# Context attention: K's fp16 parts made with keys on partitions and turned by DMA

## The chip, the core and the metric

The kernel is one program on one NeuronCore of a Trainium2 chip. Its time is the device time of that core in microseconds (us). The engines are PE (matmuls, with PEld for its weight loads), DVE (VectorE), ACT (ScalarE), POOL (GpSimd) and SP, which here only issues DMAs. Each engine works off its own list of instructions strictly in order and waits on semaphores.

## The reference, cut to what matters

Two layers, each a cross attention from 64 latent rows to a long context, a self attention and a feed-forward part. The change touches the cross attention alone, which stands in both layers. For each of 16 batches, with 16 heads of 32 channels and 1585 context keys (the last 16 of 1601 take another path):

```python
q = _ln((x @ Wq + bq).reshape(b, s1, H, HD), qn_w, qn_b)      # 64 rows, 16 heads of 32
k = _ln((y_main @ Wk + bk) by head, kn_w, kn_b)               # 1585 keys
v = y_main @ Wv + bv by head
s = einsum('bhqd,bhkd->bhqk', q, k) * SCALE
ctx = einsum('bhqk,bhkd->bhqd', softmax(s), v)
```

All of it is float32. The kernel reaches that precision with pairs of fp16 numbers: a value is its rounding to fp16 ("high") plus the fp16 of what is left ("low").

## The kernel before, in words

`context_attention` runs over 16 batches. A batch's 1585 keys are 13 tiles of 128 (the last has 49). ORDER is a table written by hand that gives each engine its steps for one turn; `batches` walks it once per batch. A step's name is its kind and its tile, and each minus sign behind it moves it one batch back, so one turn mixes the projections of one batch with the attention of the batch before it. There is one turn per batch, and what sets the order is that table alone.

The steps of one tile, in the order in which they depend on each other:

- `yh` (ACT, L335) rounds the tile's context to fp16, `yl` (DVE, L411) subtracts to get the low part. Context comes to `l_land` by two loads a batch on SP's queue (L227, L230).
- `k` and `v` (PE, L545): six matmuls of 512 columns each into `ps_k` and `ps_v`, with keys on partitions.
- `kc` (DVE, L418) takes K out of PSUM with its bias, `sq` (ACT, L341) squares it, `rd` (DVE, L426) sums by head, and for two tiles at once `r` (ACT, L347, L351) and `nw` (POOL, L270 to L279) give the reciprocal root `rstd`.
- `hat` (POOL, L287) multiplies K by it into `khat`; `kt` (PE, L566) turns khat with four float32 transposes into `ps_kt`, so that channels are on partitions.
- `kh` (ACT, L356) and `kl` (DVE, L432) split `ps_kt` into the fp16 tensors `kh` and `kl`.
- `vh` (ACT, L362) and `vl` (DVE, L439) split V.

Then, by batch: `m0` to `m12` are rough scores (PE, L583) whose maxima DVE takes (L450); `t`, `tb`, `qs`, `qh`, `ql` put the maxima into the query; `s0` to `s13` are the exact scores (PE, L617), each followed by `e` (ACT, L382 and L384: two exponentials, one to float32 and one to fp16), `lo` (POOL, L307: the difference of the two) and `pv` (PE, L641 to L645: the products with V). `m0` waits for the fp16 K of the first four tiles, `m4` and `m8` for four more each, `m12` and `s0` for all.

A wait by step: `kt` of a tile waits for `kl` of the tile before (there is one `ps_kt`), `k` for `kc` of the tile before, `v` for `vl` of it. A projection waits for the `yl` of its tile.

Of the kernel before, what the change touches and what calls it, by code (L numbers as in the profile page):

```python
# [38 lines left out]
YA = 6  # L39
# [14 lines left out]
    ACT: e9- sq11- kh7- e10- yh0 kh8- r5- vh11- e11- sq12- kh9- e12- yh1 kh10- e13- vh12- r6- kh11- sq0 yh2
    ACT: vh0 vh1 yh3 kh12- sq1 vh2 yh4 r0 sq2 qh- vh3 sq3 yh5 e0 vh4 yh6 sq4 kh0 r1 e1 vh5 yh7 sq5 kh1 e2 yh8
    ACT: vh6 sq6 r2 kh2 e3 vh7 sq7 kh3
    DVE: kc8- rd7- kl4- yl9- m0- vl8- kc9- rd8- kl5- rd9- yl10- m1- o0- vl9- kc10- yl11- rd10- kl6- m2- kc11-
    DVE: vl10- kl7- m3- yl12- rd11- kl8- m4- vl11- kc12- m5- rd12- kl9- yl0 m6- yl1 kl10- m7- kc0 vl12- kl11-
    DVE: m8- rd0 m9- vl0 yl2 kc1 m10- vl1 yl3 m11- kc2 rd1 m12- t- vl2 kc3 qs- yl4 kl12- ql- vl3 yl5 rd2 kc4
# [22 lines left out]
def context_attention(nc, env, ctx_dram, qs_dram, wk, wv, bk, wo_x_raw, dca_dram):  # L82
# [7 lines left out]
    with ExitStack() as ctx:  # L90
# [130 lines left out]

        with nc.Block() as block:

            @block.sync
            def _(sp):
                def load_a(b):
                    sp.dma_start(y[:, :, 0:YA * P], ctx_dram[b, :, :, 0:YA * P]).then_inc(y_a, 16)  # L227

                def load_b(b):
                    sp.dma_start(y[:, :, YA * P:MAIN], ctx_dram[b, :, :, YA * P:MAIN]).then_inc(y_b, 16)  # L230

                def load_q(b, bp):
                    sp.dma_start(q0[:, bp].rearrange("p g q -> p (g q)"), qs_dram[b]).then_inc(q_in[bp], 16)

                load_a(0)
                load_b(0)
                load_q(0, 0)
# [3083 lines left out]
```

## Time and profile before

| | |
|---|---|
| time, median of 3 runs | 3381.3 us (3379.84 to 3383.14) |
| span of the profiled execution | 3386.0 us |
| PE busy | 3119.5 us, 92% |
| DVE busy | 2655.1 us, 78% |
| ACT busy | 2269.3 us, 67% |
| POOL busy | 1864.8 us, 55% |

No time of the profiled execution other than its span is recorded; the span lies 4.7 us over the median of the runs. Shares are over the whole program; the two context attentions take about two thirds of it, and there the engines are busier than these shares say. The trace models the end of a matmul, and neighbouring matmuls overlap in it, so the time that a step of PE really takes is read from its start to the start of what follows. On DVE and ACT too the recorded end of an instruction lies a little behind the start of the next. Below, such a distance from start to start is called a slot.

### The profile page before, as it was taken

Reading aid. Unit: us, or ns where it says so; the run is one execution under the profiler, and the core shown is the slowest. Engines: PE = TensorE matmul, PEld = TensorE weight load, DVE = VectorE, ACT = ScalarE, POOL = GpSimd, SP = SyncE. Lnnn points to the kernel's source line nnn. Section 1 sums busy time; section 2 is a strip of 40 time slices with the busy share of each in tenths; the row PEclk is TensorE's granted clock in tenths of the full one; section 3 lists DMA queues with packets and bytes.
Section 4 is the critical chain, followed back from the end, with each engine's and each line's share of the span. In section 5 each row is a group of like instructions: output and inputs, shape, how many; then the busy total and the mean of one; then the engine's idle time right before and its main releaser. Section 6 shows DMA issues by size and latency. Waiting matters only on the chain. (4 is left out here: it accounts for less than half of the span.)

```text
span 3386.0 us, 89189 instructions
## 1 busy us (share of the span) xinstructions
PE 3119.5 (92%) x35753; PEld 1945.5 (57%) x35753; DVE 2655.1 (78%) x4082; ACT 2269.3 (67%) x4027; POOL 1864.8 (55%) x2294
## 2 busy tenths in 40 slices
PE   7799999999999968879996899999999999987889
PEld 4356665666556646667773346556655665564546
DVE  6688888888888855768875688888888888866752
ACT  5478887888788755346664468788877887774431
POOL 1267776777677742212224257677767777662310
PEclk9899999999999979989998899999999999987989
DMA  3110010101010033358884301010101001001010
GB/s 121 61 34 23 23 33 24 32 23 33 23 34 23 28 114 125 109 184 278 302 305 128 92 22 33 23 34 23 33 23 34 23 23 33 23 21 54 1 68 25
DMA packets 102368, 223.67 MB, mean 66 GB/s; under 512 B 35445, under 2 KB 47861, under 8 KB 96202
## 3 DMA queue, kind: packets, MB, share of 16 engines
q1 hardware_dynamic: 93994, 190.71, 16.9%
q0 software_dynamic: 7680, 25.17, 2.5%
q8 instruction: 289, 4.73, 0.6%
q10 hardware_dynamic: 288, 2.10, 0.1%
q14 instruction: 117, 0.96, 0.1%
HBM read 181.86 MB, written 36.09 MB: 64 GB/s over the span
## 5 line engine op out<-in xcount | busy, mean ns | idle before, releaser
L307 POOL TENSOR_TENSOR a_elo<-a_e 128x1024 f16<-128x1024 f32 x428 | 867.3, 2026 | 160.6 <-ACT a_e L384 159.6
L545 PE MATMUL a_ps_k<-l_wk,a_yh 128*128 128x512 f16 (+1 forms) x1664 | 568.3, 382 | 31.4 <-DVE a_yl L411 27.4
L545 PE MATMUL a_ps_v<-l_wv,a_yh 128*128 128x512 f16 (+1 forms) x1664 | 568.0, 382 | 19.1 <-DVE a_v L439 19.1
L450 DVE TENSOR_REDUCE a_mx<-a_ps_m 128x2 f32<-128x1024 f32 x384 | 466.7, 1215 | 13.0 <-PE a_ps_m L583 12.8
L382 ACT ACTIVATE a_e<-a_ps_t 128x1024 f32<-128x1024 f32 x428 | 410.9, 960 | 98.2 <-PE a_ps_t L617 91.8
L287 POOL TENSOR_TENSOR a_khat<-a_kc,a_rstd 128x512 f32<-128x512 f32 (+1 forms) x416 | 443.7, 1073 | 16.5 <-PE a_ps_kt L566 6.0
L384 ACT ACTIVATE a_e<-a_ps_t 128x1024 f16<-128x1024 f32 x428 | 410.7, 960 | 0.0
L411 DVE TENSOR_TENSOR a_yl<-l_land,a_yh 128x256 f16<-128x256 f32 (+1 forms) x416 | 352.0, 847 | 19.3 <-ACT a_yh L335 19.0
L418 DVE SCALAR_TENSOR_TENSOR a_kc<-a_ps_k,l_bk 128x512 f32<-128x512 f32 (+1 forms) x416 | 284.0, 683 | 91.6 <-PE a_ps_k L545 91.2
L641 PE MATMUL a_ps_o<-a_v,a_e 128*128 128x65 f16 (+1 forms) x3240 | 344.6, 194 | 10.4 <-POOL a_elo L307 10.4
L432 DVE SCALAR_TENSOR_TENSOR a_kl<-a_ps_kt,a_kh 128x512 f16<-128x512 f32 (+1 forms) x416 | 274.1, 659 | 91.2 <-ACT a_kh L356 91.2
L643 PE MATMUL a_ps_o<-a_v,a_e 128*128 128x64 f16 (+1 forms) x3240 | 343.1, 194 | 0.0
L356 ACT ACTIVATE a_kh<-a_ps_kt,a_one 128x512 f16<-128x512 f32 (+1 forms) x416 | 277.0, 666 | 96.5 <-PE a_ps_kt L566 96.4
L645 PE MATMUL a_ps_o<-a_v,a_elo 128*128 128x65 f16 (+1 forms) x3240 | 341.3, 193 | 0.0
L439 DVE SCALAR_TENSOR_TENSOR a_v<-a_ps_v,a_v 128x512 f16<-128x512 f32 (+1 forms) x416 | 284.6, 684 | 70.7 <-ACT a_v L362 68.4
L362 ACT ACTIVATE a_v<-a_ps_v 128x512 f16<-128x512 f32 (+1 forms) x416 | 246.7, 593 | 125.2 <-PE a_ps_v L545 125.2
L617 PE MATMUL a_ps_t<-a_qb,a_kh 64*128 64x128 f16 (+1 forms) x6448 | 323.9, 218 | 6.5 <-DVE a_qb L474 5.0
L641 PEld LDWEIGHTS a_ps_o<-a_v,a_e 128*128 128x128 f16 (+1 forms) x3240 | 297.8, 96 | 53.5 <-ACT a_e L384 23.1
L545 PE MATMUL a_ps_v<-l_wv,a_yl 128*128 128x512 f16 (+1 forms) x832 | 316.6, 381 | 0.0
L545 PE MATMUL a_ps_k<-l_wk,a_yl 128*128 128x512 f16 (+1 forms) x832 | 316.3, 380 | 0.0
L341 ACT ACTIVATE a_sq<-a_kc 128x512 f32<-128x512 f32 (+1 forms) x416 | 262.5, 631 | 68.5 <-DVE a_kc L418 68.5
L545 PEld LDWEIGHTS a_ps_k<-l_wk,a_yh 128*128 128x128 f16 (+1 forms) x1664 | 163.1, 98 | 249.7 <-issue 55.0
(428 smaller groups left out, 6807.2 us busy)
## 6 DMA issues: line engine op xcount, KB each, us to landing
l_ob<-in_m_w SPq DMA_DIRECT2D x32, 1024.0 KB, 8.0
l_land<-in_ctx SPq DMA_DIRECT2D x32, 817.0 KB, 5.0
l_land<-in_ctx SPq DMA_DIRECT2D x32, 768.0 KB, 4.7
f_w<-in_m_w SPq DMA_DIRECT2D x32, 512.0 KB, 4.8
eo_dram<-f_e_eo SPq DMA_DIRECT2D x32, 512.0 KB, 4.4
qs_dram<-p_q SPq DMA_DIRECT2D x32, 128.0 KB, 2.4
dca_dram<-p_od SPq DMA_DIRECT2D x16, 256.0 KB, 2.4
a_q<-qs_dram SPq DMA_DIRECT2D x32, 128.0 KB, 2.0
```

The costliest lines, as they stand in the source:

```text
L287: pool.tensor_tensor(khat[0:r, t, :].rearrange("p (h d) -> p h d", d=HD), kc[0:r, kc_slot(at, i), :].rearrange("p (h d) -> p h d", d=HD), ...
L307: pool.tensor_tensor(rest[0:r, :, 0:w], full[0:r, :, 0:w], high[0:r, :, 0:w], ALU.subtract)\
L382: act.activation(full[0:r, :, 0:w], src[0:r, :, 0:w], ACT.Exp)
L384: act.activation(high[0:r, :, 0:w], src[0:r, :, 0:w], ACT.Exp).then_inc(e_done, 1)
L411: dve.tensor_tensor(yl[:, t, :, 0:r], y[:, :, i * P:i * P + r], yh[:, t, :, 0:r], ALU.subtract).then_inc(yl_done, 1)
L439: dve.scalar_tensor_tensor(out=v[0:r, at.nbp, i, :, 66:130], in0=ps_v[0:r, :].rearrange("p (a d) -> p a d", d=64), scalar=1.0 / WSCALE, in ...
L450: dve.tensor_reduce(mx[:, g, :, c], ps_m[:, :, :], AX.X, ALU.max).then_inc(mx_done, 1)
L545: m = pe.matmul(out[0:r, :], part[:, t, c, 0:r], w[:, wpart, c, :], start=(c == 0 and a == 0), stop=(c == KC - 1 and a == 2))
L617: t = pe.matmul(dst[0:rows(i), r, col:col + P], kpart[d, at.bp, g, k], qb[d, at.bp, g, qpart, :, :].rearrange("p a q -> p (a q)"), start=( ...
L641: pe.matmul(ps_o[:, a * OW:a * OW + OW], high[k, r, col], v[k, at.bp, i, pair, 0:OW], start=first, stop=False, skip_group_check=True)
L643: pe.matmul(ps_o[:, a * OW:a * OW + 64], high[k, r, col], v[k, at.bp, i, pair, 66:130], start=False, stop=False, skip_group_check=True)
L645: t = pe.matmul(ps_o[:, a * OW:a * OW + OW], rest[k, r, col], v[k, at.bp, i, pair, 0:OW], start=False, stop=last, skip_group_check=True)
```

## The change

K's path is made anew; the other steps compute what they did.

- `hat` moves from POOL to DVE (L467 of the changed kernel). It multiplies `kc` in SBUF by the reciprocal root in PSUM and writes to PSUM: `ps_h`, which takes the place of `ps_kt`, with keys still on partitions. A new step `rp` on ACT (L384) first copies a tile's 16 reciprocal roots into the last 16 columns of `ps_h`.
- `kh` and `kl` split `ps_h` into `khl`, two buffers of [128 keys, high and low, 512 channels].
- `kt` is gone. SP issues for each tile one DMA transpose of 256 KB (64 rows for the last tile) from `khl` into `kk`, which holds high and low K with channels on partitions. `m` and `s` read `kk`, and wait for the transposes to land (`wait_turned`). `kh` of a tile waits until the transpose of two tiles before has landed; the first transpose of a batch also waits for the last scores of the batch two before.
- The split of the context (`yh`, `yl`) goes by four chunks of three tiles (the last has four), on ACT and now POOL instead of ACT and DVE: L361 and L316. The loads go by the same four chunks. A chunk's buffer is free once the V projections of the chunk two before are done.
- All four orders are written anew.

```diff
-KCOLS = MAIN + MAIN % 2
+KCOLS = -(-MAIN // 64) * 64
+RSTD = D - H
...
+CHUNKS = 4
+PER = KT // CHUNKS
+WIDEST = MAIN - (CHUNKS - 1) * PER * P + 1
...
-    PE: pv11- s13- m7- k0 kt11- pv12- pv13- m8- v0 m9- k1 m10- v1 k2 m11- kt12- v2 m12- k3 tb- v3 k4 s0 v4
+    PE: s12-- k2- pv11-- m8-- v12-- m9-- s13-- pv12-- m10-- v0- pv13-- m11-- k3- m12-- v1- tb-- k4- v2- s0-
...
+    ACT: rp11-- vh10-- r6-- kh11-- sq0- e11-- vh11-- rp12-- sq1- e12-- kh12-- r0- vh12-- e13-- yh1- sq2- rp0-
...
+    DVE: m0- kl5- kc9- hat6- rd8- m1- kc10- kl6- rd9- hat7- rd10- kl7- m2- kc11- hat8- vl7- o0- rd11- m3- kl8-
...
-        yh = sb("yh", [P, 2, KC, P], F16)
-        yl = sb("yl", [P, 2, KC, P], F16)
-        kh = sb("kh", [P, 2, GROUPS, KCOLS], F16)
-        kl = sb("kl", [P, 2, GROUPS, KCOLS], F16)
+        yh = sb("yh", [P, 2, KC, WIDEST], F16)
+        yl = sb("yl", [P, 2, KC, WIDEST], F16)
+        khl = sb("khl", [P, 2, 2, D], F16)
+        kk = sb("kk", [P, 2, 2 * GROUPS, KCOLS], F16)
...
-        ps_kt = ps("ps_kt", [P, GROUPS, P])
+        ps_h = ps("ps_h", [P, 512])
...
+        def chunk_free(eng, n):
+
+            if n >= 2:
+                b, c = divmod(n - 2, CHUNKS)
+                eng.wait_ge(v_done, b * KT + (KT if c == CHUNKS - 1 else (c + 1) * PER))
+
+        def wait_turned(eng, tiles):
+
+            for k in range(2):
+                n = len(range(k, tiles, 2))
+                if n:
+                    eng.wait_ge(turned[k], 16 * n)
...
+                def load(b, c):
+                    lo, hi = chunk_columns(c)
+                    sp.dma_start(y[:, :, lo:hi], ctx_dram[b, :, :, lo:hi]).then_inc(y_in[c], 16)
+
+                def load_q(b):
+                    sp.dma_start(q0[:, b % 2].rearrange("p g q -> p (g q)"), qs_dram[b]).then_inc(q_in[b % 2], 16)
+
+                def turn(b, i):
+                    n, r = b * KT + i, -(-rows(i) // 64) * 64
+                    sp.wait_ge(kl_done, n + 1)
+                    if i == 0 and b >= 2:
+                        sp.wait_ge(s_done, (b - 1) * UNITS)
+                    sp.dma_start_transpose(kk[:, b % 2, :, i * P:i * P + r],
+                                           khl[0:r, n % 2].rearrange("p a d -> p (a d)")).then_inc(turned[n % 2], 16)
+
+                for c in range(CHUNKS):
+                    load(0, c)
+                    if c == 0:
+                        load_q(0)
+                        load_q(1)
+                for b in range(B):
+                    for i in range(KT):
+                        if i % PER == 1 and i // PER < CHUNKS and b + 1 < B:
+                            sp.wait_ge(yl_done, b * CHUNKS + i // PER + 1)
+                            load(b + 1, i // PER)
+                        turn(b, i)
+                    if 1 <= b < B - 1:
+                        sp.wait_ge(q1_done, b)
+                        load_q(b + 1)
...
+                    need(pool, rp_done, at.nb * KT + 2 * p - 2 + (p == 0))
                     pool.tensor_tensor(rstd[0:r, u, 0:nt, :], r2, a2, ALU.mult).then_inc(newton[4], 1)
 
-                def hat(at, i):
-
-                    n, t, r, p = at.nb * KT + i, tile_par(at.nbp, i), rows(i), i // 2
-                    u = (at.nbp * TPAIRS + p) % 2
-                    pool.wait_ge(newton[4], at.nb * TPAIRS + p + 1)
-                    need(pool, kt_done, n - 1)
-                    pool.tensor_tensor(khat[0:r, t, :].rearrange("p (h d) -> p h d", d=HD),
-                                       kc[0:r, kc_slot(at, i), :].rearrange("p (h d) -> p h d", d=HD),
-                                       rstd[0:r, u, i % 2, :].unsqueeze(2).broadcast_to([r, H, HD]), ALU.mult)\
-                        .then_inc(hat_done, 1)
+                def y_low(at, c):
+                    n = at.nb * CHUNKS + c
+                    lo, hi = chunk_columns(c)
+                    pool.wait_ge(yh_done, n + 1)
+                    chunk_free(pool, n)
+                    pool.tensor_tensor(yl[:, n % 2, :, 0:hi - lo], y[:, :, lo:hi], yh[:, n % 2, :, 0:hi - lo],
+                                       ALU.subtract).then_inc(yl_done, 1)
...
+                def root_in(at, i):
+
+                    n, r, p = at.nb * KT + i, rows(i), i // 2
+                    act.wait_ge(newton[4], at.nb * TPAIRS + p + 1)
+                    need(act, kl_done, n)
+                    act.activation(ps_h[0:r, RSTD:D], rstd[0:r, (at.nbp * TPAIRS + p) % 2, i % 2, :], ACT.Copy)\
+                        .then_inc(rp_done, 1)
+
                 def k_high(at, i):
                     n, r = at.nb * KT + i, rows(i)
-                    act.wait_ge(kt_done, n + 1)
-                    act.activation(kh[:, at.nbp, :, i * P:i * P + r], ps_kt[:, :, 0:r], ACT.Identity, bias=one[:, 0:1])\
+                    act.wait_ge(hat_done, n + 1)
+                    if n >= 2:
+                        act.wait_ge(turned[n % 2], 16 * (n // 2))
+                    act.activation(khl[0:r, n % 2, 0, :], ps_h[0:r, :], ACT.Identity, bias=one[0:r, 0:1])\
                         .then_inc(kh_done, 1)
...
-                def y_low(at, i):
-                    n, t, r = at.nb * KT + i, tile_par(at.nbp, i), rows(i)
-                    dve.wait_ge(yh_done, n + 1)
-                    dve.tensor_tensor(yl[:, t, :, 0:r], y[:, :, i * P:i * P + r], yh[:, t, :, 0:r],
-                                      ALU.subtract).then_inc(yl_done, 1)
...
+                def hat(at, i):
+
+                    n, r = at.nb * KT + i, rows(i)
+                    dve.wait_ge(rp_done, n + 1)
+                    dve.tensor_tensor(ps_h[0:r, :].rearrange("p (h d) -> p h d", d=HD),
+                                      kc[0:r, kc_slot(at, i), :].rearrange("p (h d) -> p h d", d=HD),
+                                      ps_h[0:r, RSTD:D].unsqueeze(2).broadcast_to([r, H, HD]), ALU.mult)\
+                       .then_inc(hat_done, 1)
...
+                    dve.scalar_tensor_tensor(out=khl[0:r, n % 2, 1, :], in0=ps_h[0:r, :], scalar=1.0,
+                                             in1=khl[0:r, n % 2, 0, :], op0=ALU.add, op1=ALU.subtract)\
...
                 def project(at, i, out, w, done):
-                    t, r = tile_par(at.nbp, i), rows(i)
+                    c, r = chunk_of(i), rows(i)
+                    n = at.nb * CHUNKS + c
+                    pe.wait_ge(yl_done, n + 1)
+                    cols = slice((i - c * PER) * P, (i - c * PER) * P + r)
                     steps = [(yh, 0), (yl, 0), (yh, 1)]
                     for c in range(KC):
...
-                def k_turned(at, i):
-                    n, t = at.nb * KT + i, tile_par(at.nbp, i)
-                    pe.wait_ge(hat_done, n + 1)
-                    need(pe, kl_done, n)
-                    for g in range(GROUPS):
-                        m = pe.transpose(ps_kt[:, g, :], khat[:, t, g * P:(g + 1) * P], ident[:, :])
-                    m.then_inc(kt_done, 1)
-
                 def first_scores(at, m):
 
                     c, g = divmod(m, GROUPS)
-                    pe.wait_ge(kh_done, at.nb * KT + min(4 * c + 4, KT))
+                    wait_turned(pe, at.nb * KT + min(4 * c + 4, KT))
...
-                                          kh[q, at.nbp, g, o:o + w], start=True, stop=True)
+                                          kk[q, at.nbp, g, o:o + w], start=True, stop=True)
...
-                        pe.wait_ge(kl_done, at.b * KT + KT)
+                        wait_turned(pe, at.b * KT + KT)
```

PE (rows as the program has them, before), layer 0, where the last rough scores of a batch stand among projections of the next; a_ps_kt is K being turned, a_ps_m the rough scores, a_ps_k and a_ps_v the projections:

```order
L583 MATMUL a_ps_m<-a_kh,a_qm 128x512 x2
L566 MATMUL a_ps_kt<-ident,a_khat 128x128 x4
L545 MATMUL a_ps_v<-l_wv,a_yh 128x512
L545 MATMUL a_ps_v<-l_wv,a_yl 128x512
L545 MATMUL a_ps_v<-l_wv,a_yh 128x512 x2
L545 MATMUL a_ps_v<-l_wv,a_yl 128x512
L545 MATMUL a_ps_v<-l_wv,a_yh 128x512
L583 MATMUL a_ps_m<-a_kh,a_qm 128x49 x8
```

The same place in the change, m11, k3, m12 of its order:

```order
L617 MATMUL a_ps_m<-a_kk,a_qm 128x512 x2
L591 MATMUL a_ps_k<-l_wk,a_yh 128x512
L591 MATMUL a_ps_k<-l_wk,a_yl 128x512
L591 MATMUL a_ps_k<-l_wk,a_yh 128x512 x2
L591 MATMUL a_ps_k<-l_wk,a_yl 128x512
L591 MATMUL a_ps_k<-l_wk,a_yh 128x512
L617 MATMUL a_ps_m<-a_kk,a_qm 128x49 x8
```

The four transposes have gone, and the projection that stands there is k3, the first that reads the second chunk of the context.

DVE before, from m9 to m11 of a batch; a_yl is the low context:

```order
L450 TENSOR_REDUCE a_mx<-a_ps_m 128x2
L439 SCALAR_TENSOR_TENSOR a_v<-a_ps_v,a_v 128x8x64
L411 TENSOR_TENSOR a_yl<-l_land,a_yh 128x256
L418 SCALAR_TENSOR_TENSOR a_kc<-a_ps_k,l_bk 128x512
L450 TENSOR_REDUCE a_mx<-a_ps_m 128x2
L439 SCALAR_TENSOR_TENSOR a_v<-a_ps_v,a_v 128x8x64
L411 TENSOR_TENSOR a_yl<-l_land,a_yh 128x256
L450 TENSOR_REDUCE a_mx<-a_ps_m 128x2
```

DVE in the change, from the last hat of a batch on; a_ps_h is the normed K, a_khl its low part:

```order
L467 TENSOR_TENSOR a_ps_h<-a_kc,a_ps_h 49x512
L493 TENSOR_REDUCE a_mx<-a_ps_m 128x2
L475 SCALAR_TENSOR_TENSOR a_khl<-a_ps_h,a_khl 49x512
L493 TENSOR_REDUCE a_mx<-a_ps_m 128x2
L482 SCALAR_TENSOR_TENSOR a_v<-a_ps_v,a_v 49x8x64
L452 SCALAR_TENSOR_TENSOR a_kc<-a_ps_k,l_bk 128x512
L493 TENSOR_REDUCE a_mx<-a_ps_m 128x2
L467 TENSOR_TENSOR a_ps_h<-a_kc,a_ps_h 128x512
L493 TENSOR_REDUCE a_mx<-a_ps_m 128x2
L482 SCALAR_TENSOR_TENSOR a_v<-a_ps_v,a_v 128x8x64
L475 SCALAR_TENSOR_TENSOR a_khl<-a_ps_h,a_khl 128x512
```

The subtractions of the context have left DVE, and a multiplication for each tile has come in front of each low part, with one or two other instructions between the two.

SP before, one batch; a_q is the query:

```order
L233 DMA a_q<-qs_dram 128x256
L227 DMA l_land<-in_ctx 128x2x768
L230 DMA l_land<-in_ctx 128x2x817
L233 DMA a_q<-qs_dram 128x256
L227 DMA l_land<-in_ctx 128x2x768
```

SP in the change, one batch:

```order
L263 DMA_TRANSPOSE a_kk<-a_khl 128x8x128
L253 DMA l_land<-in_ctx 128x2x384
L263 DMA_TRANSPOSE a_kk<-a_khl 128x8x128 x3
L253 DMA l_land<-in_ctx 128x2x384
L263 DMA_TRANSPOSE a_kk<-a_khl 128x8x128 x3
L253 DMA l_land<-in_ctx 128x2x384
L263 DMA_TRANSPOSE a_kk<-a_khl 128x8x128 x3
L253 DMA l_land<-in_ctx 128x2x433
L263 DMA_TRANSPOSE a_kk<-a_khl 128x8x128 x2
L263 DMA_TRANSPOSE a_kk<-a_khl 128x8x64
L256 DMA a_q<-qs_dram 128x256
```

Thirteen transposes have come into the queue of the loads, which stand between them.

## Rows read from the trace of the kernel before

**Rows 1.** the page: the span and the busy time of each engine

```profile
span 3386.0 us, 89189 instructions
...
PE 3119.5 (92%) x35753; PEld 1945.5 (57%) x35753; DVE 2655.1 (78%) x4082; ACT 2269.3 (67%) x4027; POOL 1864.8 (55%) x2294
```

**Rows 2.** windows, one turn: busy us PE, PEld, DVE, ACT, POOL; clock, DMA

```profile
501.70:570.24 68.54, 67.43 (x897) 40.66 (x897) 59.71 (x89) 54.37 (x97) 51.06 (x64) 1.00 0.09 28
```

**Rows 3.** timeline of PE: start us, us, engine, line, op, shapes, count

```profile
513.10 0.38 PE L545 MATMUL a_ps_k<-l_wk,a_yh 128*128 128x512 f16 x1
...
514.49 0.39 PE L583 MATMUL a_ps_m<-a_kh,a_qm 64*128 64x512 f16 x2
514.81 0.65 PE L566 MATMUL a_ps_kt<-ident,a_khat 128*128 128x128 f32 x4
515.30 0.38 PE L545 MATMUL a_ps_v<-l_wv,a_yh 128*128 128x512 f16 x1
```

**Rows 4.** timeline of PE, same turn: the longest and the shortest transpose step

```profile
523.99 0.60 PE L566 MATMUL a_ps_kt<-ident,a_khat 128*128 128x128 f32 x4
524.67 0.38 PE L545 MATMUL a_ps_k<-l_wk,a_yh 128*128 128x512 f16 x1
...
532.82 0.60 PE L566 MATMUL a_ps_kt<-ident,a_khat 128*128 128x128 f32 x4
533.25 0.19 PE L641 MATMUL a_ps_o<-a_v,a_e 128*128 128x65 f16 x1
```

**Rows 5.** timeline of PE where the last batch of layer 0 starts its scores

```profile
1204.49 0.39 PE L617 MATMUL a_ps_t<-a_qb,a_kh 64*128 64x128 f16 x4 [2.48 <-DVE a_qb L474]
```

**Rows 6.** the score line L617: count, duration ns min/median/max, first and last start us

```profile
L617 PE MATMUL a_ps_t<-a_qb,a_kh x6448: 216/216/312, 179.2 to 3049.2; 64*128 64x128 f16 x179, 64*49 64x128 f16 x17
```

**Rows 7.** DVE over that turn by line: count, busy us, mean ns, idle before

```profile
L450 DVE TENSOR_REDUCE a_mx<-a_ps_m 128x2 f32<-128x1024 f32 x13 | 15.8, 1215 | 0.3 <-PE a_ps_m L583 0.3
L411 DVE TENSOR_TENSOR a_yl<-l_land,a_yh 128x256 f16<-128x256 f32 (+1 forms) x13 | 11.4, 876 | 0.0
...
L432 DVE SCALAR_TENSOR_TENSOR a_kl<-a_ps_kt,a_kh 128x512 f16<-128x512 f32 (+1 forms) x13 | 8.6, 659 | 2.7 <-ACT a_kh L356 2.7
```

**Rows 8.** ACT over the same turn, by line

```profile
L384 ACT ACTIVATE a_e<-a_ps_t 128x1024 f16<-128x1024 f32 (+1 forms) x15 | 14.4, 962 | 0.0
...
L335 ACT ACTIVATE a_yh<-l_land 128x256 f16<-128x256 f32 (+1 forms) x13 | 5.3, 408 | 1.6 <-PE a_ps_v L545 1.6
...
L351 ACT ACTIVATE a_r<-a_lnv 128x32 f32<-128x32 f32 (+1 forms) x7 | 1.6, 227 | 0.6
```

**Rows 9.** POOL over the same turn, by line

```profile
L307 POOL TENSOR_TENSOR a_elo<-a_e 128x1024 f16<-128x1024 f32 (+1 forms) x14 | 28.3, 2023 | 3.8 <-ACT a_e L384 3.8
L287 POOL TENSOR_TENSOR a_khat<-a_kc,a_rstd 128x512 f32<-128x512 f32 (+1 forms) x14 | 15.1, 1085 | 0.3
```

**Rows 10.** timeline of DVE: L411 beside a POOL instruction and alone, with what follows

```profile
571.00 2.16 DVE L411 TENSOR_TENSOR a_yl<-l_land,a_yh 128x256 f16<-128x256 f32 x1
573.08 0.68 DVE L432 SCALAR_TENSOR_TENSOR a_kl<-a_ps_kt,a_kh 128x512 f16<-128x512 f32 x1
...
580.13 0.41 DVE L411 TENSOR_TENSOR a_yl<-l_land,a_yh 128x256 f16<-128x256 f32 x1
580.46 0.68 DVE L418 SCALAR_TENSOR_TENSOR a_kc<-a_ps_k,l_bk 128x512 f32<-128x512 f32 x1
581.06 1.21 DVE L450 TENSOR_REDUCE a_mx<-a_ps_m 128x2 f32<-128x1024 f32 x1
```

**Rows 11.** timeline of POOL at the first of the two

```profile
570.75 2.12 POOL L307 TENSOR_TENSOR a_elo<-a_e 128x1024 f16<-128x1024 f32 x1
```

**Rows 12.** DMA issues of the page: count, KB each, median us to landing

```profile
qs_dram<-p_q SPq DMA_DIRECT2D x32, 128.0 KB, 2.4
dca_dram<-p_od SPq DMA_DIRECT2D x16, 256.0 KB, 2.4
```

**Rows 13.** DMA issues by line, further down: another transfer of 256 KB

```profile
h_dram<-f_h SPq DMA_DIRECT2D x8, 256.0 KB, 12.2
```

More of the change, by code:

```diff
@@ L54 @@
[L54 to L59, printed above, removed]
@@ L60 @@
-    DVE: rd3 o1- vl4 yl6 kc5 kl0 rd4 vl5 rd5 kl1 yl7 kc6 vl6 kl2 rd6 kc7 yl8 vl7 kl3
-    POOL: hat4- lo3- hat5- lo4- nw3- lo5- hat6- lo6- hat7- lo7- nw4- lo8- hat8- lo9- hat9- lo10- nw5- hat10-
-    POOL: lo11- hat11- lo12- lo13- nw6- hat12- qm nw0 hat0 hat1 lo0 nw1 lo1 hat2 hat3 lo2 nw2
+    PE: k12-- v8-- pv7-- s9-- m4-- pv8-- v9-- k0- s10-- m5-- v10-- k1- pv9-- m6-- s11-- v11-- pv10-- m7--
+    PE: s12-- k2- pv11-- m8-- v12-- m9-- s13-- pv12-- m10-- v0- pv13-- m11-- k3- m12-- v1- tb-- k4- v2- s0-
@@ new lines @@
+    ACT: r4- kh7- e7-
+    DVE: kc2- m10-- hat0- m11-- vl0- kl0- m12-- t-- kc3- rd2- qs-- vl1- rd3- hat1- ql-- kc4- kl1- vl2- kc5-
+    DVE: hat2- rd4- vl3- kl2- o1-- kc6- rd5- hat3- vl4- rd6- kl3- kc7- hat4- vl5- rd7- kl4- kc8- hat5- vl6-
+    DVE: m0- kl5- kc9- hat6- rd8- m1- kc10- kl6- rd9- hat7- rd10- kl7- m2- kc11- hat8- vl7- o0- rd11- m3- kl8-
+    DVE: kc12- vl8- hat9- m4- kl9- vl9- hat10- kc0 m5- kl10- rd12- hat11- vl10- kc1 kl11- m6- rd0 m7- vl11-
+    DVE: rd1 hat12- m8- kl12- m9- vl12-
@@ L63 @@
+    POOL: nw0- lo13-- yl1- nw1- yl2- qm- lo0- lo1- nw2- lo2- yl3- lo3- nw3- lo4- lo5- lo6- nw4- lo7- lo8- yl0
+    POOL: nw5- lo9- lo10- nw6- lo11- lo12-
 """
@@ L134, in context_attention @@
         ps_o = ps("ps_o", [P, 512])
-        y_a, y_b, const_ok, ones_ok = sem("y_a"), sem("y_b"), sem("const_ok"), sem("ones_ok")
+        const_ok, ones_ok = sem("const_ok"), sem("ones_ok")
+        y_in = [sem(f"y_in{c}") for c in range(CHUNKS)]
         q_in = [sem("q_in0"), sem("q_in1")]
@@ L171, in context_attention @@
         e_sets = [(e32[:, t], e16[:, t], elo[:, t]) for t in range(2)]
-        for t, spare in enumerate((khat, sq)):
-            halves = spare[:, :, :].bitcast(F16).rearrange("p t (u n) -> p (t u) n", n=512)
-            e_sets.append((kc[:, 2 * t:2 * t + 2], halves[:, 0:2], halves[:, 2:4]))
+        halves = sq[:, :, :].bitcast(F16).rearrange("p t (u n) -> p (t u) n", n=512)
+        e_sets.append((kc[:, 0:2], khl[:, 0], khl[:, 1]))
+        e_sets.append((kc[:, 2:4], halves[:, 0:2], halves[:, 2:4]))
         def e_set(at, j):
@@ L213, in batches @@
         def batches(name, attention, step):
-            for turn in range(-2, B + 1):
+            for turn in range(-2, B + 2):
                 for kind, i, shift in STEPS[name]:
@@ L225, in _ @@
             def _(sp):
[L226 to L237, printed above, removed]
@@ L312, in step @@
                         newton_step(at, i)
-                    elif kind == "hat":
-                        hat(at, i)
+                    elif kind == "yl":
+                        y_low(at, i)
                     elif kind == "qm":
@@ L361, in v_high @@
                     act.wait_ge(v_done, n + 1)
+                    if i == 0 and at.nb >= 2:
+                        act.wait_ge(pv_done, 2 + (at.nb - 1) * UNITS)
                     act.activation(v[0:r, at.nbp, i, :, 0:64], ps_v[0:r, :].rearrange("p (a d) -> p a d", d=64),
@@ L392, in step @@
                         guess(at, i)
+                    elif kind == "rp":
+                        root_in(at, i)
                     elif kind == "kh":
@@ L508, in step @@
                 def step(kind, i, at):
-                    if kind == "yl":
-                        y_low(at, i)
-                    elif kind == "kc":
+                    if kind == "kc":
                         k_centred(at, i)
+                    elif kind == "hat":
+                        hat(at, i)
                     elif kind == "rd":
@@ L544, in project @@
                         for a, (part, wpart) in enumerate(steps):
-                            m = pe.matmul(out[0:r, :], part[:, t, c, 0:r], w[:, wpart, c, :],
+                            m = pe.matmul(out[0:r, :], part[:, n % 2, c, cols], w[:, wpart, c, :],
                                           start=(c == 0 and a == 0), stop=(c == KC - 1 and a == 2))
@@ L653, in step @@
                         v_product(at, i)
-                    elif kind == "kt":
-                        k_turned(at, i)
                     elif kind == "m":
```

60 lines of the change are left out of this document (22 added, 38 removed).

## The prediction

> **What bounds the kernel now.** I read the busy shares first, then one turn of a context attention, then the slots of PE in it. Over the program PE is busy 92% of 3386.0 us [rows 1]. In one turn of layer 0 (68.54 us) PE is busy 67.43 us at the full granted clock of 1.00, DVE 59.71, ACT 54.37 and POOL 51.06 [rows 2]. So PE sets the pace and DVE comes 13% behind it. The length of a turn is fixed from outside too: the first exact scores start at 179.2 us [rows 6] and those of the last batch at 1204.49 [rows 5], 15 turns apart, so 68.35 us each. Two layers make 30 such turns, 2050 of the 3386 us. What one turn gains counts 30 times; the rest of the program is untouched but for the filling and draining of each attention.
>
> **PE: the transposes go.** A transpose step (four float32 matmuls) takes from its start to the next start 0.49 us in the middle of projections (514.81 to 515.30) [rows 3], at most 0.68 and at least 0.43 [rows 4]. The 13 of the turn have a mean of 0.51, so 13 x 0.51 = 6.6 us go from PE (5.6 and 8.8 if all were like the shortest or the longest). Nothing replaces them on PE: the matmuls of k, v, m, s and pv are the same in number and shape. If every other wait of PE stayed, a turn would be 68.35 - 6.6 = 61.7 us. The matmuls of a k step take 1.39 us up to the next start (513.10 to 514.49) and an m step 0.32 [rows 3].
>
> **DVE: subtraction out, multiplication in.** Thirteen subtractions leave, 11.4 us [rows 7], some 10.4 without the overlaps of about 0.08 us between neighbours. They are dear because POOL holds them up: alone one has a slot of 0.33 us (580.13 to 580.46), but the one that starts at 571.00 takes until 573.08 [rows 10], while POOL's 570.75 instruction runs for 2.12 us [rows 11]. Thirteen multiplications of 512 columns with PSUM on one side come in. The nearest row is kc, also 512 columns from PSUM with a second operand in SBUF: a slot of 0.60 us (580.46 to 581.06) [rows 10], so 7.8 us. The other end is a multiplication held up as the subtractions are, 0.876 us each [rows 7], 11.4 us. I take 0.60. DVE then has 59.7 - 10.4 + 7.8 = 57.1 us of work in a turn of some 62 to 63, 91% against 87% now.
>
> The trace's pair of subtractions shows the hold-up by its 0.33 and 2.08 us. The Trainium skill (SBUF — State Buffer, "Who interferes with whom") says that a DVE instruction with two inputs in SBUF contends with a GpSimd instruction that reads SBUF, and one with a single SBUF input doesn't; the trace agrees for the subtraction, and the multiplication is of the second kind, since the roots are copied to PSUM. By this rule it costs 0.60; without it the 0.876 would stand, 3.6 us a turn more on DVE.
>
> **ACT and POOL.** ACT loses 13 roundings, 5.3 us (4.3 without overlaps). It gains four of 768 to 866 columns, which by the exponential of 1024 columns in 0.962 us [rows 8] are 0.75 to 0.85 each, 3.1 in all, and 13 copies of 16 columns, bounded by zero and by the 0.227 us of a 32-column instruction [rows 8]: 2.5. ACT goes from 54.4 to 55.7 us. POOL loses khat (15.1 us for the 14 that fall in the window [rows 9], 14.1 for 13) and gains 3170 columns of subtraction, at 2.12 us for 1024 [rows 11] 6.6 us: 43.6 us. Neither sets a turn, but both stand in chains.
>
> **A new wait of PE: k3.** The second chunk of the context may be rounded only when the V projections of tile 12 of the batch before are done, and k3 needs its low part. In ACT's order the rounding yh1 stands behind e13, in POOL's yl1 behind lo13. From the end of v12 PE has m9, s13, pv12, m10, v0, pv13, m11 before k3; three m at 0.32 and v0 at 1.3 make 2.3, and the two pv and s13 come to some 1.7: 4.0 us. The other side: s13 ends at 0.8, two exponentials of half size (by 0.962 for a full one, some 0.55 each) end at 2.0, lo13 (half of 2.12) at 3.2, yl1 (768 columns, 1.6) at 4.8, and a semaphore later PE may go on, at about 5.0. So PE waits 1.0 us once a turn; the bounds are 0 and 2. Before k0 and k6 and k9 the same sum leaves PE no wait.
>
> **The transposes.** The trace has none; its price is bounded by other DMAs. Below: 256 KB of plain rows land in 2.4 us, and 128 KB in 256-byte pieces also in 2.4 [rows 12]. A transpose moves 1024 pieces of 256 bytes, twice as many, so between 2.4 and 4.8 by these two. Above: another 256 KB transfer took 12.2 us [rows 13], eight of them queued behind each other. I take 3.5, in the middle of the near rows. Who waits: kh of a tile waits for the transpose of two tiles before, and a tile comes every 62.8 / 13 = 4.8 us, so two buffers leave about 9.6 less the 1.5 of kh and kl, 8 us. Tighter are the rough scores. Between kl3 and the maximum m0, DVE has eight instructions with a slot of about 0.60, 4.8 us; less PE's own m0 (0.3) and a semaphore, the transpose may take 4.3 us. Between kl11 and m8 the same count gives 4.3; before m4 and m12, 7 and 6. At 3.5 none is late, but the margin is under one microsecond at two places. Behind a late m on PE stand the exact scores and behind these the exponentials, so a late transpose counts in full. Behind a waiting transpose on SP stand only loads that are due a whole turn later; their four 400 KB transfers a turn are issued between transposes.
>
> How the chip treats a transpose no row here can show. The Trainium skill says of the crossbar that "TRN2 transpose DMAs are as fast as regular DMAs" (Advanced Engine Details and Errata, "X-Bar Transpose (TRN2)"), which would be 2.4 us by our plain row and leave the sum as it is. The same page calls the transpose efficiency of hardware descriptor generation "Worse" than that of the software way ("DGE: Hardware vs Software") and gives no figure; this is the kind used here, and it speaks for the slower rival below.
>
> **The sum.** A turn: 68.35 - 6.6 + 1.0 = 62.8 us, 5.6 less (I round up); 30 turns, -168 us. The ends: filling is nearest to DVE's work, which falls by 2.6 us in each layer, -5; in draining the last transpose must land before m12, +3.5 in each, +7. Together -166, from 3386.0 to 3220 of span. The profiled execution lies 4.7 us over the median of the runs, so I forecast 3215 us.
>
> **Rivals.**
> - *DVE and the chains take over.* A tile of K now goes ACT, DVE, ACT, DVE through the one ps_h: copy, multiply, round, subtract, four handovers where before there were three. If DVE keeps the 8.8 us of idle time that it has in a turn now [rows 2], a turn is 57.1 + 8.8 = 65.9, 2.5 less: 3386 - 75 - 5 = 3306. For it: kl waits 2.7 us a turn for kh [rows 7], and three engines stand near 90% at once. Against it: much of that idle time is there because PE is late, and the new order puts one or two instructions between hat and kl. A multiplication that is held up by POOL (3.6 us) would end here too.
> - *Transposes land late: slower.* The place is PE before m0 and m8, then m4 and m12. With a landing time of L us each turn pays (L - 4.3) twice, (L - 5.9) and (L - 7.2) where positive. That eats the gain of 5.6 at L = 6.7; at 8 it is 10.3, so 4.7 a turn longer: 3381 + 141 = 3522. At 12.2 it would be about 27 a turn, and the ring of two buffers alone would give (1.2 + 12.2) / 2 x 13 = 87 us a turn: about 3940. For it: 416 transposes through one queue, pieces of 256 bytes, loads in between. Against it: DMA engines are busy 9% in a turn now [rows 2].
> - *PE loses its other waits too.* The order is new, k3 needn't wait, and PE's 1.1 us of idle time [rows 2] goes: 68.35 - 6.6 - 1.1 = 60.7, 7.7 less: 3381 - 231 = 3150. It needs DVE at 94%.
>
> **How the numbers follow.** Forecast 0.50 (3180 to 3260: 61.7 to 64.3 a turn); DVE and chains 0.18, near 3306; no other waits 0.10, near 3150; late transposes 0.22, of which 0.19 slower than before and 0.03 level with it. So faster by over 0.2% 0.78, within 0.2% (about what runs of this kernel can tell from no change) 0.03, slower 0.19. The range from 3155 to 3350 leaves out most of the late transposes (0.16) and a little below (0.03).
>
> **What would show it.** A turn of 62.8 us between the first exact scores of two batches; no float32 transposes on PE; the multiplication at 0.60 us a slot; POOL's subtraction of a chunk near 1.6 us; a wait of about 1 us before k3 for POOL; transposes that land in 3 to 4 us, and no wait of m for a DMA. It is wrong if m or kh waits for transposes by microseconds, if DVE is over 93% busy, or if the turn is over 65 us with PE idle for DVE or ACT.

## The result, and the profile after

The changed kernel takes 3176.5 us (median of 4 runs, 3169.9 to 3177.5) against 3382.2 us for the kernel before on the same chip: a ratio of 0.9382, 95% interval 0.937 to 0.9393, 206 us faster. The forecast was 3215 in a range of 3155 to 3350. The measured time lies in the range, but 3.5 us below the band of 3180 to 3260 that the forecast gave its own mechanism. In a later group of runs the same kernel gave 0.9374 (0.9361 to 0.9386). The span of the profiled execution is 3175.6 us, 210.4 less than before [rows 1].

The page of the changed kernel, its span and busy times, the answer to [rows 1]:

```profile
span 3175.6 us, 86675 instructions
...
PE 2894.2 (91%) x34089; PEld 1765.8 (56%) x34089; DVE 2585.9 (81%) x4082; ACT 2282.1 (72%) x4155; POOL 1619.6 (51%) x2006
```

One turn of its layer 0, the answer to [rows 2] (length, busy us and count of PE, PEld, DVE, ACT, POOL, clock, DMA share, GB/s):

```profile
547.24:608.40 61.16, 59.97 (x845) 35.06 (x844) 57.07 (x89) 54.73 (x100) 43.35 (x54) 1.00 0.46 85
```

The first exact scores of the first and of the last batch of layer 0, which fix the length of 15 turns as [rows 5, 6] do for before:

```profile
183.17 0.84 PE L651 MATMUL a_ps_t<-a_qb,a_kk 64*128 64x128 f16 x24 [0.43 <-DVE a_qb L517]
```

```profile
1100.69 1.46 PE L651 MATMUL a_ps_t<-a_qb,a_kk 64*128 64x128 f16 x24 [2.48 <-DVE a_qb L517]
```

A turn is (1100.69 - 183.17) / 15 = 61.17 us, where it was 68.35. (Most turns are 61.30 us from first score to first score, where they were 68.54; the last of a layer is shorter.) Thirty turns give 7.18 x 30 = 215 us, and 5 are given back at the ends: the first scores start 4.0 us later than before (183.2 against 179.2). DVE's 57.07 and POOL's 43.35 us are the forecast's 57.1 and 43.6; ACT has 54.73, forecast 55.7.

The lines of DVE in that turn that answer to [rows 7], and of ACT and POOL to [rows 8, 9]:

```profile
L493 DVE TENSOR_REDUCE a_mx<-a_ps_m 128x2 f32<-128x1024 f32 x12 | 14.6, 1218 | 0.2 <-PE a_ps_m L617 0.2
...
L467 DVE TENSOR_TENSOR a_ps_h<-a_kc,a_ps_h 128x512 f32<-128x512 f32 (+1 forms) x13 | 8.9, 687 | 1.8 <-ACT a_ps_h L384 1.7
L475 DVE SCALAR_TENSOR_TENSOR a_khl<-a_ps_h,a_khl 128x512 f16<-128x512 f32 (+1 forms) x13 | 8.9, 681 | 0.6 <-ACT a_khl L392 0.4
```

```profile
L361 ACT ACTIVATE a_yh<-l_land 128x768 f16<-128x768 f32 (+1 forms) x4 | 3.4, 860 | 0.0
L384 ACT ACTIVATE a_ps_h<-a_rstd 128x16 f32<-128x16 f32 (+1 forms) x13 | 2.5, 189 | 1.9 <-DVE a_khl L475 1.9
```

```profile
L317 POOL TENSOR_TENSOR a_yl<-l_land,a_yh 128x768 f16<-128x768 f32 (+1 forms) x4 | 6.5, 1637 | 0.8 <-ACT a_yh L361 0.7
```

The multiplication costs 687 ns, like kc. The order's extra instruction between hat and kl shows too: DVE waits 0.4 us a turn for kh, where it waited 2.7 [rows 7]. It now waits 1.7 for the copies of the roots; in all it is idle for 4.1 us of the turn, where it was for 8.8 [rows 2]. The DMA issues of the page, which answer to [rows 12, 13], have the transposes in them:

```profile
a_kk<-a_khl SPq DMA_TRANSPOSE x416, 3.1
qs_dram<-p_q SPq DMA_DIRECT2D x32, 128.0 KB, 2.3
dca_dram<-p_od SPq DMA_DIRECT2D x16, 256.0 KB, 2.4
```

A transpose of 256 KB lands after a median of 3.1 us (2.7 to 5.3 over 416 of them), 0.7 more than the plain transfer. It takes the DMA engines longer than that suggests: they are busy 46% of the turn against 9%, with 85 GB/s against 28. No m of the turn waits for one. From the end of kl to the m that needs it the trace has 5.9 us before m0 (561.4 to 567.3), where the forecast counted 4.3; 4.5 before m8 (594.4 to 598.9), where it counted 4.3; and 6.7 and 5.8 before m4 and m12, where it had 7 and 6. So only m8 is tight. The place in PE's order where the forecast saw a new wait (start, length, what, and the idle time with its releaser):

```profile
543.49 0.39 PE L617 MATMUL a_ps_m<-a_kk,a_qm 64*128 64x512 f16 x2
544.24 0.38 PE L591 MATMUL a_ps_k<-l_wk,a_yh 128*128 128x512 f16 x1 [0.36 <-POOL a_yl L317]
```

k3 does wait for POOL's yl1, but 0.4 us, not 1.0.

### The profile page after: what moved, and what is told of

Its sections match the earlier page's. It is cut to its first block and busy times, and to the rows that moved or that the text cites. A ratio compares the mean times of both kernels' runs of the same rounds, so it can differ in the third digit from the quotient of the medians.

```text
span 3175.6 us, 86675 instructions
## 1 busy us (share of the span) xinstructions
PE 2894.2 (91%) x34089; PEld 1765.8 (56%) x34089; DVE 2585.9 (81%) x4082; ACT 2282.1 (72%) x4155; POOL 1619.6 (51%) x2006
## 5 line engine op out<-in xcount | busy, mean ns | idle before, releaser
L335 POOL TENSOR_TENSOR a_elo<-a_e 128x1024 f16<-128x1024 f32 x428 | 852.9, 1996 | 301.4 <-ACT a_e L422 297.7
L651 PE MATMUL a_ps_t<-a_qb,a_kk 64*128 64x128 f16 (+1 forms) x9672 | 350.5, 218 | 23.0 <-DVE a_qb L517 20.2
L675 PEld LDWEIGHTS a_ps_o<-a_v,a_e 128*128 128x128 f16 (+1 forms) x3240 | 298.6, 96 | 98.5 <-issue 61.5
L651 PEld LDWEIGHTS a_ps_t<-a_qb,a_kk 64*128 64x128 f16 (+1 forms) x9672 | 286.4, 95 | 103.7 <-DVE a_qb L517 35.4
L467 DVE TENSOR_TENSOR a_ps_h<-a_kc,a_ps_h 128x512 f32<-128x512 f32 (+1 forms) x416 | 285.8, 687 | 58.1 <-ACT a_ps_h L384 55.7
L677 PEld LDWEIGHTS a_ps_o<-a_v,a_e 128*128 128x128 f16 (+1 forms) x3240 | 299.8, 97 | 24.8
L392 ACT ACTIVATE a_khl<-a_ps_h,a_one 128x512 f16<-128x512 f32 (+1 forms) x416 | 284.0, 683 | 33.1 <-DVE a_ps_h L467 32.1
L679 PEld LDWEIGHTS a_ps_o<-a_v,a_elo 128*128 128x128 f16 (+1 forms) x3240 | 300.2, 99 | 0.0
L475 DVE SCALAR_TENSOR_TENSOR a_khl<-a_ps_h,a_khl 128x512 f16<-128x512 f32 (+1 forms) x416 | 283.4, 681 | 19.2 <-ACT a_khl L392 12.6
```

The source lines that it names most:

```text
L335: pool.tensor_tensor(rest[0:r, :, 0:w], full[0:r, :, 0:w], high[0:r, :, 0:w], ALU.subtract)\
L392: act.activation(khl[0:r, n % 2, 0, :], ps_h[0:r, :], ACT.Identity, bias=one[0:r, 0:1])\
L467: dve.tensor_tensor(ps_h[0:r, :].rearrange("p (h d) -> p h d", d=HD), kc[0:r, kc_slot(at, i), :].rearrange("p (h d) -> p h d", d=HD), ps_h ...
L651: t = pe.matmul(dst[0:rows(i), r, col:col + P], kk[d, at.bp, kpart + g, k], qb[d, at.bp, g, qpart, :, :].rearrange("p a q -> p (a q)"), st ...
L675: pe.matmul(ps_o[:, a * OW:a * OW + OW], high[k, r, col], v[k, at.bp, i, pair, 0:OW], start=first, stop=False, skip_group_check=True)
L677: pe.matmul(ps_o[:, a * OW:a * OW + 64], high[k, r, col], v[k, at.bp, i, pair, 66:130], start=False, stop=False, skip_group_check=True)
```

## The experiments

All times are compared through their ratio to the kernel before on the same chip, with the changed kernel at 0.9374 to 0.9382. One per cent is 34 us. "Over 15 turns" means from the first exact scores of the first batch of layer 0 to those of its last, as above.

**PE's transposes put back.** In `k_product` of the changed kernel:

```diff
                     need(pe, kc_done, at.nb * KT + i)
+                    for g in range(GROUPS):
+                        pe.transpose(ps_k[:, g * P:(g + 1) * P], ident[:, :], ident[:, :])
                     project(at, i, ps_k, wk, k_done)
```

> The changed kernel with four float32 transposes of the identity put on PE in front of every k step, into ps_k, where the matmuls of k overwrite them: PE gets back what it lost and nothing else changes. Theory (PE sets the pace of a turn, and its transposes were the gain): 13 x 0.5 = 6.6 us a turn, 30 turns, about +200 us, so 3360 to 3390, the time before. Rival (part of the gain comes from DVE's dear subtractions having gone, and PE has slack): under +130 us, below 3310.

Measured: 3331.0 us, ratio 0.9827 (0.981 to 0.9843), 151 us slower than the changed kernel: between the two, nearer to the rival. One turn of it:

```profile
513.45:579.86 66.41, 66.11 (x897) 41.20 (x897) 57.65 (x89) 55.34 (x100) 43.52 (x54) 1.00 0.41 78
```

Over 15 turns a turn is 66.18 us, 5.0 longer than the changed kernel's. Its k steps, with the transposes in them, take 6.1 us more slots than the changed kernel's (23.6 against 17.5 us), and PE's idle time shrinks by 0.9 us (1.2 to 0.3). With as many transposes as before, PE still finishes a turn 2.2 us earlier than in the kernel before (68.35); up to 0.5 of that may be the transposes themselves, which took 6.6 us of slots there.

**The kernel before with its transposes doubled.**

```diff
-                    for g in range(GROUPS):
+                    for g in (0, 1, 2, 3, 0, 1, 2, 3):
```

> The kernel before with every K tile turned twice on PE, eight transposes instead of four: if a turn was bound by PE alone, 13 x 0.45 to 0.51 = 5.9 to 6.6 us a turn, 3385 + 177 to 200 = 3560 to 3590. If PE had slack for part of them: below 3540.

Measured: 3541.3 us, ratio 1.0459 (1.0442 to 1.0477), 155 us slower, at the edge of the second reading. It is the same price from the other side: over 15 turns a turn is 73.41 us, 5.1 longer. Its kt steps took 5.4 us more slots (12.0 against 6.6). So in both kernels the slots of the step overstate what it costs the turn.

**Less work on PE, DVE and ACT, one by one and together.** In this order: V's low product (the two matmuls of six that read `yl`), half of the columns of the 12 large maxima, half of the fp16 exponential. The last also sets the fp16 buffer to zero once on POOL at the start.

```diff
-                    steps = [(yh, 0), (yl, 0), (yh, 1)]
+                    steps = [(yh, 0), (yh, 1)] if w is wv else [(yh, 0), (yl, 0), (yh, 1)]
...
-                        dve.tensor_reduce(mx[:, g, :, c], ps_m[:, :, :], AX.X, ALU.max).then_inc(mx_done, 1)
+                        dve.tensor_reduce(mx[:, g, :, c], ps_m[:, :, 0:256], AX.X, ALU.max).then_inc(mx_done, 1)
...
-                    act.activation(high[0:r, :, 0:w], src[0:r, :, 0:w], ACT.Exp).then_inc(e_done, 1)
+                    h = w // 2 if at.b < B - 1 else w
+                    act.activation(high[0:r, :, 0:h], src[0:r, :, 0:h], ACT.Exp).then_inc(e_done, 1)
```

> The changed kernel without the product of the low part of the context in the V projections: two matmuls of six fewer for each of 13 tiles, 26 x 0.216 = 5.6 us of PE a turn; the low part of V's input is left out of the result. Theory (PE alone sets the pace still): -5.6 x 30 = -168, near 3010. Rival (PE, DVE and ACT are now all near the turn's length, DVE has 57.0 of 61.2 us): the turn cannot fall below DVE's 57 us plus its waits, so -2 a turn at most, 3110 or above.

> The changed kernel with the 12 large maxima of a turn taken over half of their columns (half of the keys left out of the maximum): about 12 x 0.53 = 6.4 us less on DVE, the same order. If PE alone sets the pace: only the waits of PE for DVE go (k3's and the one before s0, about 1 us a turn), 3140 to 3180. If DVE sets it as much: -3 us a turn or more, 3080 or below.

> The changed kernel with the fp16 exponential taken over half of its columns in all batches but a layer's last (the other half keeps old values, so part of the probabilities is left out): 14 x 0.37 = 5.2 us less on ACT of the turn's 54.7, same order. PE less by 5.6 us gave only 0.4 us a turn and DVE less by 6.4 gave 0.3. Theory (the three in-order lists hold each other: one engine less leaves the other two and the handovers): another 0.2 to 1 us a turn, 3145 to 3175. Rival (ACT has become the bound through its waits): -3 us a turn or more, 3090 or below.

> The three reliefs together: V's low product out on PE (-5.6 us a turn), maxima over half the columns on DVE (-6.4), half of the fp16 exponential on ACT (-5.2). Theory (balanced engines): together they give far more than the sum of the single gains of about 1 us: 3 to 5 us a turn, 3030 to 3090. Rival (a fixed chain of handovers or of the transposes sets the turn at about 60.5 us): under 2 us a turn, above 3115.

Measured, with the gain over the changed kernel:

| | us | ratio (95%) | gain |
|---|---|---|---|
| PE less | 3153.3 | 0.9304 (0.9289 to 0.932) | 24 to 26 |
| DVE less | 3156.0 | 0.9311 (0.9295 to 0.9326) | 21 to 24 |
| ACT less | 3167.6 | 0.9357 (0.9337 to 0.9377) | 6 to 9 |
| all three | 3046.4 | 0.8992 (0.8977 to 0.9007) | 129 to 132 |

Turns of the kernel with less on PE and of the one with less on all three:

```profile
539.73:600.47 60.74, 56.29 (x818) 32.28 (x818) 56.98 (x89) 54.48 (x101) 43.38 (x54) 1.00 0.46 85
```

```profile
513.63:570.83 57.20, 54.92 (x820) 32.11 (x819) 51.11 (x89) 49.10 (x100) 43.37 (x54) 1.00 0.54 90
```

PE alone gives up 3.7 us of busy time and the turn 0.4 (0.6 over 15 turns). Over 15 turns DVE alone gives 0.5 us a turn and ACT alone 0.25, but the three together 3.9, three times the sum; over the whole program it is still more than twice. No single engine bounds the changed kernel: PE, DVE and ACT do jointly, each strictly in order and waiting for the others within a turn. One relief alone would have misled: the run with less on DVE came out where it was expected if PE alone set the pace (3140 to 3180), and only the one with less on PE excludes that. The gain with all three also says that no chain of transposes holds the turn at 60.

**The kernel before with less on DVE.** The same edit of the maxima in the kernel before.

> The kernel before with its 12 large maxima of a turn over half of their columns: 6.4 us less on DVE of 59.7, PE and the order as they were. It tells whether DVE's load cost the kernel before anything, as putting PE's transposes back into the changed kernel left it 50 us faster. If yes (waits of PE for DVE): -1 to -2 us a turn, 3320 to 3355. If the 50 us come from the new orders: within 0.5 us a turn, 3370 or above.

Measured: 3346.8 us, ratio 0.9885 (0.9869 to 0.9902), 40 us faster. Over 15 turns a turn is 67.28 us, so DVE's load did cost the kernel before 1.1 us a turn; the rest of the 40 us is at the ends (the first scores start 4.0 us earlier). In the trace the gain is for the most part PE's own idle time, which falls from 1.1 to 0.35 us a turn. By steps, counted with the waits in front of what follows, it is in m with tb (4.6 us of slots instead of 5.2) and in v (17.7 instead of 18.1).

**The roots read from SBUF.** In `hat`; the guard of the buffer of the roots on POOL then waits for `hat` instead of the copy.

```diff
-                                      ps_h[0:r, RSTD:D].unsqueeze(2).broadcast_to([r, H, HD]), ALU.mult)\
+                                      rstd[0:r, (at.nbp * TPAIRS + i // 2) % 2, i % 2, :].unsqueeze(2).broadcast_to([r, H, HD]), ALU.mult)\
```

> The changed kernel with the multiplication on DVE reading the reciprocal roots from SBUF instead of PSUM, so that both inputs are in SBUF; the copy on ACT stays and is waited for as before. Theory (a DVE instruction with two inputs in SBUF is held up while POOL reads SBUF): the mean of the multiplication goes from 0.69 to 0.9 to 1.5 us, DVE over 60 us a turn, and the time rises by 60 to 250 us. Rival (the subtractions were dear for another reason, their float32 and fp16 inputs): mean stays within 0.1 us of 0.69 and the time within 0.3%.

Measured: 3493.9 us, ratio 1.031 (1.0293 to 1.0328): 315 us slower than the changed kernel, slower than before. The multiplication in this kernel and in the changed one (duration ns min/median/max):

```profile
L467 DVE TENSOR_TENSOR a_ps_h<-a_kc,a_rstd x416: 680/1586/2657, 117.3 to 3121.0; 128x512 f32<-128x512 f32 x128, 49x512 f32<-49x512 f32 x11
```

```profile
L467 DVE TENSOR_TENSOR a_ps_h<-a_kc,a_ps_h x416: 674/685/697, 118.6 to 2802.7; 128x512 f32<-128x512 f32 x128, 49x512 f32<-49x512 f32 x11
```

With one operand moved its minimum stays 0.68 us and its median becomes 1.59. That it is POOL that holds it up shows when the 384 full multiplications of this run are sorted: the 50 that overlap no POOL instruction of over 0.4 us take 0.68 to 0.70 us, the 334 others 1.74 in the median. In the changed kernel both kinds take 0.69. The copy of 16 roots to PSUM, 0.19 us on ACT, is what makes the change pay at all: of all the edits tried here, leaving it unused cost most.

**Transposes issued later.** In SP's `turn`:

```diff
                     sp.wait_ge(kl_done, n + 1)
+                    sp.wait_ge(hat_done, min(n + 2, B * KT))
```

> The changed kernel with each transpose issued only when the multiplication of the next tile is done too, 1.7 to 2.6 us after its own low part: a transpose is in effect 5 us long instead of 3.1. By the margins of the forecast (4.3 us before m0 and m8) each turn pays about 0.8 us twice: +1.6 us a turn, +30 to +60 us. Rival (the margins are wider than the sum of slots, since DVE and PE wait in between): within 10 us. If the two buffers of khl hold up ACT: +100 us or more.

Measured: 3389.1 us, ratio 1.0 (0.999 to 1.001): 212 us slower, the whole gain gone. The delay was larger than the expectation had it: between kl11 and hat12 DVE's order has m6, rd0, m7, vl11 and rd1. DVE in this kernel around tile 11: its low part (L476), the next tile's multiplication (L468), and the maximum of m8 (L494):

```profile
573.01 0.67 DVE L476 SCALAR_TENSOR_TENSOR a_khl<-a_ps_h,a_khl 128x512 f16<-128x512 f32 x1
...
577.73 0.68 DVE L468 TENSOR_TENSOR a_ps_h<-a_kc,a_ps_h 49x512 f32<-49x512 f32 x1
582.32 1.23 DVE L494 TENSOR_REDUCE a_mx<-a_ps_m 128x2 f32<-128x1024 f32 x1 [3.91 <-PE a_ps_m L618]
```

PE at the same place:

```profile
577.05 0.38 PE L592 MATMUL a_ps_k<-l_wk,a_yh 128*128 128x512 f16 x1
581.67 0.61 PE L618 MATMUL a_ps_m<-a_kk,a_qm 64*128 64x512 f16 x2 [3.46 <-issue]
582.21 0.62 PE L592 MATMUL a_ps_v<-l_wv,a_yh 128*49 128x512 f16 x1
582.63 0.63 PE L592 MATMUL a_ps_v<-l_wv,a_yl 128*49 128x512 f16 x1
```

The transpose of tile 11 is issued after 578.4 instead of 573.7, 4.7 us late, and with 3.1 us to land it is there at 581.5; m8 starts at 581.67. As a transpose of 4.7 + 3.1 = 7.8 us against the forecast's margin of 4.3 before m8, it should cost 3.5 us: PE waits 3.46. So the margin before m8 was right. The wait of 0.8 us expected before m0 as well isn't there: tile 3 is issued 1.8 us after its low part, but the margin there is 5.9 us and not 4.3. This turn is 68.4 us, 7.1 longer than the usual 61.3 (turns of this run vary by over 2 us; over 15 turns the mean is 67.8). Of the 7.1, m8 takes 3.5, and m12, which waits for its tile in the same way, 1.1. Another 1.2 is v12, which runs at half the clock: PE stood idle for 3.46 us before m8, the granted clock is then 0.50 (the level of 1.2 GHz) from 581.5 to 584.5, and a matmul of 512 columns follows the last after 0.42 us (582.21 to 582.63) instead of 0.22. Where the remaining 1.4 us go was not followed up.

The whole turn, and the stretch behind the wait (the number before the DMA share is the granted clock):

```profile
525.49:593.89 68.40, 62.23 (x846) 35.34 (x845) 57.44 (x89) 54.67 (x100) 43.38 (x54) 0.98 0.39 76
...
581.60:583.60 2.00, 1.93 (x6) 0.74 (x7) 1.28 (x2) 0.00 (x0) 0.04 (x1) 0.50 0.00 0
```

**Two exchanges in the orders**, to take the waits that the trace of the changed kernel shows before s0 and k3. The first alone, then both, beside the changed kernel itself:

```diff
-    DVE: kc2- m10-- hat0- m11-- vl0- kl0- m12-- t-- kc3- rd2- qs-- vl1- rd3- hat1- ql-- kc4- kl1- vl2- kc5-
+    DVE: kc2- m10-- hat0- m11-- vl0- kl0- m12-- t-- kc3- rd2- qs-- vl1- rd3- ql-- hat1- kc4- kl1- vl2- kc5-
...
-    PE: s12-- k2- pv11-- m8-- v12-- m9-- s13-- pv12-- m10-- v0- pv13-- m11-- k3- m12-- v1- tb-- k4- v2- s0-
+    PE: s12-- k2- pv11-- v12-- m8-- m9-- s13-- pv12-- m10-- v0- pv13-- m11-- k3- m12-- v1- tb-- k4- v2- s0-
```

> The changed kernel with one pair exchanged in DVE's order, ql before hat1: in the trace PE waits 0.5 us for ql before s0 of every batch, and ql could start 0.6 us earlier. If that wait is on the path: -0.5 x 30 = -15 us against the changed kernel. If the engines are balanced, as the reliefs say, the delay of hat1, kh1 and kl1 gives part of it back: 0 to -6 us.

> As the one before, and on PE v12 ahead of m8, so that the V projection that frees the context's buffer ends 0.3 us earlier and k3, which waits 0.4 us a turn, gets its input earlier; m8 comes 1.3 us later. If both waits go and nothing else becomes late: -25 us against the changed kernel. If m8's maximum is then late on DVE: no gain beyond the exchange on DVE, or some us lost.

> The changed kernel itself, on the same chip as the three others of this group, to compare them with: 0.937 to 0.940 of the kernel before.

Measured: 3191.3 us, ratio 0.9417 (0.9404 to 0.943); 3242.5, ratio 0.9563 (0.955 to 0.9576); the changed kernel 3176.8, ratio 0.9374 (0.9361 to 0.9386). Both exchanges made it slower, by 15 and 66 us: the first against both expectations, the second by far more than the few us expected. In the first, DVE waits 3.1 us a turn for the copies of the roots instead of 1.7, ACT 1.6 for the multiplications instead of 0.8: the wait before s0 for ql went and came back along K's chain. In the second, the trace shows a new wait of 1.4 us in every turn: both m8 and m9 now stand behind v12, and m9 waits for DVE to take the maximum of m8. That is the whole difference between the two (most turns take 63.28 and 61.85 us), and k3 still waits 0.4 for POOL, so the exchange on PE did nothing for it. No version tried beats the changed kernel.

## Why the prediction was right, and where its terms were off

- *PE's transposes, 6.6 us a turn.* The mechanism was right, the size was not: putting them back costs 5.0 us and doubling them before 5.1. The slots were real, but PE's other waits took up about 1 us of them.
- *Nothing for DVE's relief and the new orders.* This is the term that was missing. With PE's work restored, the changed kernel is still 1.7% faster than before, 59 us, and its turn 2.2 us shorter. The kernel before gained 1.1 us a turn from a lighter DVE, so it had such waits to lose. How the 2.2 us divide between DVE's 2.5 us less work, the subtractions that POOL no longer holds up and the orders was not tried apart.
- *The wait before k3, +1.0.* The mechanism and the releaser were right, its size 0.4. yl1 ended 4.7 us after v12, as forecast (4.8), but PE came to k3 after 4.5 us of work instead of 4.0. Two small waits, before m10 and v0, are 0.24 of that; the rest is slots longer than counted.
- *DVE's multiplication at 0.60 us, ACT, POOL.* Right; the SBUF experiment shows that the other end of the bound was no worst case, for there the mean is 1.585 us and not the 0.876 that the forecast put there.
- *The transposes, 3.5 us and late nowhere.* Right in the turns, at 3.1 us, with the margins given above. The ends together cost 5 us instead of 2: the first scores of layer 0 start 4.0 us later, where the forecast had the filling 2.6 shorter. Why was not looked into.
- *The sum.* 5.6 us a turn forecast, 7.2 measured: 5.0 for the transposes and 2.2 for the rest, where the forecast had 6.6 less 1.0. The first term was 1.6 too large and the second 3.2 too small, so it is in part luck that the sum came as near as it did. Thirty turns make 47 us of difference. The ends take 3 of them back. The offset between span and median takes another 6: the forecast took 4.7 us off the span, where the measured median lies 0.9 above it. That leaves the 39 us.
- *The rivals.* The one with DVE and the chains in charge (65.9 us a turn, 3306 as a span) let DVE keep its 8.8 us of idle time; it kept 4.1. It was right that PE would no longer be alone: PE less by two matmuls in six gives 26 us where PE alone in charge would give 168. The forecast's own sign against it, DVE over 93% busy, is just met (57.07 of 61.16 us, 93.3%), and rightly, since DVE now shares the bound. The rival without PE's other waits (60.7 us, 3150) is about as near to the measured 61.2 and 3176.5 as the forecast, but not for its reason: PE is idle for 1.2 us of the turn, where it was for 1.1. The slower one had the margin before m8 right and the one before m0 too small by 1.6 us.

## What to carry to other kernels

In this kernel PE, DVE and ACT, all in order, stand within a tenth of each other. There the slots of a removed step overstated its gain, and a relief on the second engine was worth something before it was the bound. Both can be measured by adding the step back and by taking work off each engine, alone and together. Moving a transpose off PE to DMA paid here because its 3 us of landing fit between two steps that exist anyway; so count what the other engines do in between, at the tightest place and not in the mean. And when an elementwise operation with both inputs in SBUF moves to VectorE beside a busy GpSimd, try its small operand in PSUM: it was worth 315 us here.

## What the runs showed of the hardware that was not expected

A transpose of 256 KB in 256-byte pieces lands in 3.1 us (2.7 to 5.3 over 416 of them), yet keeps the DMA engines busy far out of proportion: 13 a turn raise their share from 9% to 46% while the bytes moved grow from 28 to 85 GB/s. And the hold-up of VectorE beside GpSimd costs more than the instruction itself: 1.59 us in the median for 0.68 us of work.
